# Graph network kernel: TensorE's order inside a group of 512 edges, with the scatter's first tile moved behind the messages

## What is computed

```python
h = jnp.maximum(_layernorm(x, axis=-1), 0.0)
nodes_i = h[vertices[:, 0]]
nodes_j = h[vertices[:, 1]]
messages = _mlp3(jnp.concatenate([nodes_i, nodes_j, edges], axis=1), mW1, mb1, mW2, mb2, mW3, mb3)
summed = segment_sum(messages, vertices[:, 0], N) + segment_sum(messages, vertices[:, 1], N)
upd_in = jnp.concatenate([h, summed, attention], axis=1)
x = x + _mlp3(upd_in, uW1, ub1, uW2, ub2, uW3, ub3)
```

## Time and profile before

| what | value |
|---|---|
| runs, median (lowest, highest) | 792.36 us (792.22, 792.84) |
| the profiled execution, own time | 792.18 us |
| its span, first to last instruction | 790.3 us |
| mean granted TensorE clock | 0.989 |
| PE busy | 759.9 us (96%) |
| PE weight loads (beside PE) | 595.4 us (75%) |
| DVE busy | 692.1 us (88%) |
| POOL busy | 545.6 us (69%) |
| ACT busy | 483.1 us (61%) |

### The profile page before, as it was taken

The page is one execution under the profiler, slowest core; times in us unless marked ns, Lnnn a source line. Parts: engine busy times, 40 slices in busy tenths (PEclk is TensorE's granted clock), DMA queues, the critical chain, the costliest instruction groups (busy, mean ns, idle before and its releaser), DMA issues.

```text
span 790.3 us, 13338 instructions
## 1 busy us (share of the span) xinstructions
PE 759.9 (96%) x4270; PEld 595.4 (75%) x4270; DVE 692.1 (88%) x1454; ACT 483.1 (61%) x642; POOL 545.6 (69%) x530
## 2 busy tenths in 40 slices
PE   4599999999999999999999999999999999998988
PEld 4367777787777787777877777877778777776857
DVE  6989999999999999999999999999999999977753
ACT  3146676666766666766667666667666676663631
POOL 2777777777777777777777777777777777772000
PEclk9889999999999999999999999999999999999999
DMA  6534443444433444434444334444344444441000
GB/s 189 158 120 127 128 127 114 121 127 125 123 116 118 123 125 127 120 111 124 127 124 124 117 117 121 127 124 123 111 126 125 122 126 124 118 124 32 1 0 27
DMA packets 42452, 90.14 MB, mean 114 GB/s; under 512 B 11024, under 2 KB 17808, under 8 KB 42384
## 3 DMA queue, kind: packets, MB, share of 16 engines
q0 software_dynamic: 24576, 67.14, 28.7%
q1 hardware_dynamic: 17808, 22.16, 9.4%
HBM read 86.64 MB, written 2.62 MB: 113 GB/s over the span
## 4 chain that ended last, share of the span: by engine, by line
PE 91%; DVE 5%; issue 1%; ACT 1%; DVEq 1%; DMA 1%; ACTq 0%
PE bank L586 29%; PE bank L565 21%; PE bank L575 14%; PE bank L553 8%; PE bank L547 8%; PE bank L596 4%; PE bank L715 2%; PE bank L674 1%; DVE oh_key L990 1%; DMA x_sb<-x 1%; DVE oh_low L989 1%; ACT dist L774 0%; PE bank L682 0%; PE bank L668 0%; DVE inc L941 0%
## 5 line engine op out<-in xcount | busy, mean ns | idle before, releaser
L413 POOL DMA_INDIRECT tab_sb<-table_a,ends_i x256 | 277.6, 1084 | 80.0 <-issue 77.7
L421 POOL DMA_INDIRECT tab_sb<-table_b,ends_i x256 | 258.7, 1011 | 78.0 <-issue 78.0
L941 DVE TENSOR_SCALAR inc<-dist,half_gap,times 128x1026 fp32r<-128x1026 f16 (+1 forms) x256 | 275.5, 1077 | 28.4 <-ACT dist L774 25.2
L774 ACT ACTIVATE dist<-iota_h,neg_mid 128x1026 f16<-128x1026 f16 (+1 forms) x256 | 292.7, 1145 | 0.0
L764 ACT ACTIVATE h_sb<-bank,b_sb 128x512 f32<-128x512 f32 x128 | 87.6, 684 | 184.4 <-PE bank L565 184.4
L586 PE MATMUL bank<-inc,m_hi 128*128 128x512 f32 x512 | 170.7, 414 | 0.3 <-DVE inc L941 0.3
L586 PE MATMUL bank<-inc,m_lo 128*128 128x512 f32 x512 | 160.9, 395 | 0.0
L990 DVE TENSOR_SCALAR oh_key<-iota_h,key_f,minus_base 128x258 bf16<-128x258 f16 x330 | 131.3, 398 | 0.0
L575 PE MATMUL bank<-w_sb,h_sb 128*128 128x128 f32 x1024 | 125.0, 275 | 0.2
L575 PEld LDWEIGHTS bank<-w_sb,h_sb 128*128 128x128 f32 x1024 | 119.4, 192 | 1.1 <-ACT h_sb L764 1.1
L758 ACT ACTIVATE h_hi<-bank 128x512 fp32r<-128x512 f32 x128 | 75.8, 593 | 69.2 <-PE bank L553 69.2
(11 more groups left out here) (163 smaller groups left out, 566.3 us busy)
## 6 DMA issues: line engine op xcount, KB each, us to landing
e_raw<-edge_attr_t SPq DMA_DIRECT2D x128, 128.0 KB, 3.2
tab_sb<-table_a,ends_i POOLq DMA_INDIRECT x256, 2.8
tab_sb<-table_b,ends_i POOLq DMA_INDIRECT x256, 3.0
table_a<-tab_sb SPq DMA_DIRECT2D x1, 1024.0 KB, 4.9
table_b<-tab_sb SPq DMA_DIRECT2D x1, 1024.0 KB, 4.8
x_sb<-x SPq DMA_DIRECT2D x1, 512.0 KB, 4.3
w_sb<-mW SPq DMA_DIRECT2D x2, 256.0 KB, 4.6
out<-oh_key SPq DMA_DIRECT2D x4, 128.0 KB, 1.8
```

The lines of the kernel that those rows point to most:

```text
L413: nc.gpsimd.indirect_dma_start(got[:, b, t, 0, :], None, table_a, bass.IndirectOffsetOnAxis(ap=ends_i[:, 0, tile:tile + 1], axis=0),).then ...
L421: nc.gpsimd.indirect_dma_start(got[:, b, t, 1, :], None, table_b, bass.IndirectOffsetOnAxis(ap=ends_i[:, 1, tile:tile + 1], axis=0),).then ...
L774: nc.scalar.activation(to, of, ACT.Abs, bias=neg_mid[:, bass.ds(g * GT + t, 1)]).then_inc(dist_ready, 1)
L941: nc.vector.tensor_scalar(to, of, half_gap[:, tile], times[:, tile], ALU.is_equal, ALU.mult).then_inc(inc_ready, 1)
```

## The change

TensorE's program for a group is written in another order. Before, tile 0 of the scatter stands between the transposes of half 0 and those of half 1. Now both halves' transposes follow each other, then come the messages and the window, and then all four tiles of the scatter. Group 62 keeps its order.

```diff
                 if nxt:
                     first_layer(g + 1, 1 - b, i + b, 0)
-                if past and not more:
-                    scatter(g - 1, 1 - b, 0)
-                if nxt:
                     first_layer(g + 1, 1 - b, i + b, 1)
                 if now and not more:
                     messages(g)
                 if b == 1 and summed_in(i):
                     window(i + 1)
                 if past:
-                    scatter(g - 1, 1 - b, 1)
-                    scatter(g - 1, 1 - b, 2)
-                    scatter(g - 1, 1 - b, 3)
+                    for t in range(1 if more else 0, GT):
+                        scatter(g - 1, 1 - b, t)
```

## The result

The changed kernel takes 794.86 us (median of 18 runs, 792.51 to 796.67), the kernel before, run beside it 18 times, 792.64 us (791.87 to 793.49). The ratio is 1.0025 with an interval from 1.0016 to 1.0034: 1.3 to 2.7 us slower. The forecast was 792.7 us and no change, with a range from 790.8 to 795.0. The time lies inside the range, near its upper end. The change, 0.25%, is a little above the 0.2% that I had called no change; the interval, 0.16 to 0.34%, holds both answers.

A forecast was written before the change was run, and what follows sets the result against it. TensorE, busy 96% of the span, was taken to bound the kernel. Terms of -0.6 and +0.9 us gave +0.3 us on the profiled 792.18 us; with the median 0.18 us higher, the forecast was 792.7 us, range 790.8 to 795.0.

The forecast's parts named there:

- Term 1: TensorE, groups 1 to 61: same matmuls reordered, only seam prices change; -0.01 us a group, -0.6 us in all.
- R1: Rival: the first scatter pair's seam is a real cost, saved in every group; 787.8 us, chance 0.07.
- Term 2: Group 63: tile 0 no longer fills TensorE's wait for ACT's relu and follows the messages; +0.9 us.
- Waits that the change moves, costed at nothing: Earlier messages keep 0.88 us of room; DVE waits about 0.3 us for tile 0 in odd groups, covered; no cost.
- R2: Rival: DVE's 0.3 us lag in odd groups is not made up and reaches TensorE; 801 us, chance 0.06.
- The sum: Whole kernel: -0.6 + 0.9 = +0.3 us on the profiled 792.18 us; median forecast 792.7 us.
- R4: Rival: TensorE's clock falls to half in each run of eight transposes; 61 us more, 854 us, chance 0.01.
- The rule of the Trainium skill: TensorE: transposes don't count as busy like other matmuls, so longer runs could let the clock fall; forecast followed the trace.
- R3: Rival: messages wait for ACT's second relu in every group; 799 us at 0.1 us each, chance 0.05.

The follow-up runs named there:

- f0: The changed kernel run again with no further edit; 794.25 us, ratio 1.0016 to the kernel before.
- f3: Changed kernel, but tile 0 ahead of the messages in group 63 and POOL's large addition put off until all sums are there; 792.2 us, ratio 0.9993.
- h2: Changed kernel, but order of before in groups 61 and 63 and POOL's large addition put off; 791.06 us, ratio 0.9986 to the kernel before.
- g4: Kernel before, with the change in group 63 alone (tile 0 behind the messages); 925.54 us, ratio 1.0034, ScalarE held up.
- first trace: Trace of the changed kernel itself, from a run of its lower clump of times; 792.51 us.
- g1: Changed kernel, but order of before in groups 61 and 63 and POOL's large addition put off; 933.8 us, ratio 1.0114, ScalarE held up.
- g2: Changed kernel, but order of before in groups 61 and 63, POOL's addition left where it was; 935.58 us beside 924.62, ScalarE held up.
- g3: Changed kernel plus 8 never-read matmuls ahead of the counting loop; 941.02 us beside 924.62 for the kernel before, ScalarE held up.
- h1: Changed kernel plus 8 never-read matmuls ahead of the counting loop, run again; 935.8 us beside 926.83, ScalarE held up.
- e0: The changed kernel run again with no further edit; 918.83 us beside 919.14 for the kernel before, ScalarE held up.
- e3: Changed kernel, but tile 0 ahead of the messages in group 63 and POOL's large addition put off; 917.0 us beside 919.14, ScalarE held up.

## Why the prediction was right and wrong

- **Term 1, the seams: right, but 0.8 us came on top.** Eight transposes in one run take 0.93 us, as group 0's row had said, and the 0.55 us of the first scatter pair were no cost of a seam. R1 with its 5.5 us is out. The gain over 61 groups is 1.40 us where I had 0.6. From the transposes to the next second layer the mean over 56 steady groups is shorter by 0.01 us, as worked out. What came on top lies elsewhere: 0.02 us in the second layer behind each odd group (2.83 to 2.81), some 0.6 us in all, and 0.24 us in an early group (10.56 to 10.32 us between edge products, 0.07 to 0.12 in f0, f3 and h2). I had both at nothing; what shortens the second layer is not known.
- **Term 2, the last group: right.** +0.94 us on the way from the last messages to the bias in all traces that have the late tile 0 in group 63, g4 among them, and gone in all that don't.
- **"Waits that the change moves, costed at nothing": the step that was wrong.** I worked out DVE's wait of 0.3 us and its cover for a steady odd group, and both came out so (0.31 us at 410.30, no wait of TensorE behind it). But I took one group for all 31. Group 61 is another case: no one-hots stand ahead, so DVE comes earlier and would wait 1.25 us; and the loop that TensorE waits for follows with no cover in between. It is the same mechanism as in R2, at one place and not in 31. In the changed kernel itself this wait doesn't show, since POOL's addition, for which I had no term at all, holds DVE's `inc` longer: from group 62's edge products to the `inc` of tile 0 it is 6.64 us, with the late tile 0 alone 6.09, before 4.94. Together they cost 1.6 us, more than all that the steady groups had gained.
- **The sum.** -1.4 + 1.6 + 0.9 is +1.1 us, where I had said +0.3. That the time came out inside my range is in part luck: term 1 was too small, the waits were missing, and the two errors have opposite signs. The measured difference is 2.2 us in the medians, and the rest, about 1 us, isn't fully explained. I had put the clock at nothing, going by slices that count as 9 all that is 90% or more; these can hide the piece at half clock that the kernel before has at 769 us. In the first trace a piece of 1.0 us appears behind 731 us and one of 1.6 us at 769 us is gone, in f0's trace another 1.0 us is lost in the counting loop, and 1.1 us at the start. How often each comes, the traces can't say. R4 had the clock fall in the runs of transposes of groups 1 to 61: from 60 to 700 us the granted clock is 1.00 in the traces of the changed kernel, f0, f3 and h2. The rule of the Trainium skill that I had weighed against the trace (page "TensorE: Matmul & The Clock Gate", section "PE-mode transpose") cost nothing there: runs of eight transposes between other matmuls took 0.93 us there.
- **R3, the messages wait for ScalarE**, is in no group but 63 where ScalarE runs freely. Where it was held up, four kernels with the new order in the steady groups took 1.0107 to 1.0166 times the kernel before, each interval above 1.005 (g1, g2, g3, h1), and g4 with the old order 1.0034 (0.9995 to 1.0074). The session of e0 to e3 doesn't bear this out: their ratios of 1.010 to 1.014 rest on two of the eleven runs of the kernel before, and the medians of all runs lie 0 to 0.4% below its median. The waits of g1 and of g4:

```profile
PE bank L576 <- ACT h_sb L765: 70.2, 44, 3.5
DVE inc L942 <- PE bank L587: 63.5, 27, 4.5
```

```profile
PE bank L575 <- ACT h_sb L767: 63.3, 45, 3.5
```

The messages wait somewhat more in g1, and DVE's wait for tile 0 is 63.5 us, where g4 has 2.0 and the changed kernel with a free ScalarE 10.4. So it looks as if the new order gives less room to a late engine; which of the two waits makes the 1%, if either does, was not tried.

## What to carry to other kernels

Work out a moved step in the first and last rounds of a pipeline as well as in the middle: an engine whose side work has ended comes earlier and meets waits that the steady rounds cover. A gain on the engine that bounds the kernel also moves all that follows the last round; look at what now lies beside what, above all large GpSimd operations beside fast DVE ones. And a tile of independent work between two dependent steps is room for a late partner: it can be moved at no cost where it covers nothing, and costs its full length where it filled a hole, as in group 63.

## What I had not expected of the hardware

- A DVE `tensor_scalar` of 0.81 us took 2.70 us beside a GpSimd addition of 2.39 us, another form of the same operation its usual 1.34 us. In six traces the held instruction ended 0.56 or 0.57 us after the addition, wherever inside it it had begun.
- The pieces at half clock in the tail change place between executions. Behind the wait of 2.7 us for the pair sums in group 62 the clock fell in the first trace and in h2, and not in the kernel before and in f3, where that wait is the same; the first two had no piece near 769 us (2.05 us instead of 3.53 for the same 16 matmuls), the other two had one.
- In three of five sessions ScalarE stood still for 5 to 7 us at a time and all kernels took 16 to 19% longer; h1 and h2 ran on the same chip, the one with and the other without it. A change of 0.3% can't be timed so, but distances inside the trace could still be read.
